# Attention heads computed transposed, with denominators from a block of ones

## The reference

```python
# x: (64, 64, 128); HEADS = 8, DIM_QK = 64, dv = 16, n = 64
qk = x @ W_qk
q, k = jnp.split(qk, 2, axis=-1)
v = x @ W_v
...
dots = jnp.einsum('bhid,bhjd->bhij', q, k) * SCALE
bias = conv[:, dist]
attn = jax.nn.softmax(dots + bias[None], axis=-1)
out = jnp.einsum('bhij,bhjd->bhid', attn, v)
out = out.transpose(0, 2, 1, 3).reshape(b, n, h * dv)
return out @ W_out + b_out
...
x = _layernorm(x + _L0_attn_ref(...), axis=-1)
```

## Time and profile before

| | |
|---|---|
| median of 3 runs | 484.66 us |
| lowest, highest | 481.88, 485.7 us |
| profiled execution, its own time | 484.01 us |
| its span in the trace | 482.3 us |
| mean granted TensorE clock | 0.975 of full speed |
| instructions in the span | 14464 |

### The profile page before, as it was taken

One profiled execution on the slowest core, in us unless ns is written; L12 is line 12 of the kernel. 1 busy time (PEld: TensorE's weight loads), 2 busy tenths in 40 slices (PEclk: granted clock), 3 DMA queues, 4 the chain that ended last, 5 costly groups with the idle time before them and its releaser, 6 DMA issues.

```text
span 482.3 us, 14464 instructions
## 1 busy us (share of the span) xinstructions
PE 446.0 (92%) x5114; PEld 377.0 (78%) x5115; DVE 308.0 (64%) x993; ACT 301.1 (62%) x675; POOL 185.6 (38%) x209
## 2 busy tenths in 40 slices
PE   8999999999988999999889999988888999899984
PEld 7688888888877767666558999887877999899631
DVE  5578888888886578878875687433333544445246
ACT  5677877787675989978678745443435664232236
POOL 5522022208100111127556556366564666554300
PEclk9999999999998999999988999998898999999998
DMA  5342226700000061111121242122212232211186
GB/s 143 88 125 77 77 59 125 212 3 3 12 14 24 23 220 46 45 34 59 56 72 47 80 116 78 29 68 66 75 56 72 71 82 79 79 51 35 56 302 199
DMA packets 47485, 38.05 MB, mean 79 GB/s; under 512 B 5056, under 2 KB 40784, under 8 KB 47424
## 3 DMA queue, kind: packets, MB, share of 16 engines
q1 hardware_dynamic: 42672, 28.10, 21.2%
q0 software_dynamic: 4320, 8.92, 5.6%
q10 hardware_dynamic: 432, 0.20, 0.2%
HBM read 19.30 MB, written 16.34 MB: 74 GB/s over the span
## 4 chain that ended last, share of the span: by engine, by line
PE 54%; DVE 21%; ACT 10%; issue 6%; another core or an unknown queue 3%; DMA 3%; DVEq 1%; SPq 0%; ACTq 0%; POOL 0%; POOLq 0%
PE bank L1418 9%; PE bank L1332 6%; PE bank L1376 4%; PE bank L1386 3%; PE bank L1405 3%; PE bank L1407 2%; PE bank L1406 2%; DVE tkr L1541 2%; DVE negmax L1550 2%; DVE prob L1547 2%; PE bank L1056 2%; PE bank L1003 2%; PE bank L1005 2%; PE bank L1004 2%
## 5 line engine op out<-in xcount | busy, mean ns | idle before, releaser
L593 POOL DMA_INDIRECT routed<-rh,zbuf x71 | 74.1, 1043 | 60.5 <-DVE rh L1926 34.7
L1926 DVE TENSOR_SCALAR rh<-bank,zbuf 128x128 f32<-128x128 f32 x71 | 24.8, 349 | 53.2 <-PE bank L1418 20.2
L1418 PE MATMUL bank<-wdn,prob 128*128 x400 | 52.0, 285 | 1.1 <-issue 1.0
L1418 PEld LDWEIGHTS bank<-wdn,prob 128*128 128x128 f32 x400 | 49.8, 201 | 1.7 <-issue 1.4
L928 ACT ACTIVATE prob<-bank 128x512 f32<-128x512 f32 x50 | 29.3, 597 | 25.9 <-remote 12.0
L1405 PE MATMUL bank<-xT_hi,wq_hi 128*128 128x256 f32 x100 | 31.6, 316 | 9.9 <-ACT prob L928 7.4
L490 POOL DMA_INDIRECT slots<-zbuf,slot x32 | 31.7, 989 | 21.9 <-PE bank L1332 8.7
L490 POOL DMA_INDIRECT slots<-tkr,slot x32 | 31.6, 989 | 12.4 <-issue 6.7
L480 POOL TENSOR_TENSOR hlw<-hst,lnw 128x512 f32<-128x512 f32 x8 | 10.2, 1274 | 63.2 <-ACT hst L803 63.2
L913 ACT ACTIVATE prob<-bank 128x512 f32<-128x512 f32 x21 | 12.5, 597 | 31.1 <-PE bank L1376 29.1
L1332 PEld LDWEIGHTS bank<-sdn,qblk 128*128 128x128 f32 x256 | 30.1, 194 | 0.6
(11 more groups left out here) (303 smaller groups left out, 1228.6 us busy)
## 6 DMA issues: line engine op xcount, KB each, us to landing
slots<-x2T SPq DMA_DIRECT2D x8, 585.0 KB, 5.2
zbuf<-slots SPq DMA_DIRECT2D x25, 130.0 KB
tkr<-in_x SPq DMA_DIRECT2D x8, 256.0 KB, 3.1
cs<-in_ctx SPq DMA_DIRECT2D x8, 256.0 KB, 2.9
wup<-in_L_ffn_routed_up SPq DMA_DIRECT2D x1, 2048.0 KB, 8.4
zbuf<-tkr SPq DMA_DIRECT2D x8, 256.0 KB
wup<-routed SPq DMA_DIRECT2D x8, 256.0 KB, 3.7
wdn<-routed SPq DMA_DIRECT2D x8, 256.0 KB, 4.3
```

What stands on the lines that cost most here:

```text
L593: pool.indirect_dma_start(routed, bass.IndirectOffsetOnAxis(ap=xr[n][:, :].bitcast(I32)[:, DEST:DEST + 1], axis=0), yr[n % 4][:, :], None) ...
L1418: m = mm(bank[6 + a][:, 0:D], hTp[:, q, c // 2, c % 2, a, :], wdn[:, bass.ds(e * (FC * D) + c * D, D)], start=(c == 0), stop=(c == FC - 1))
L1926: tsc(yr[n % 4][:, :], bank[6 + n % 2][:, 0:D], xr[n % NX][:, GATE:GATE + 1], None, ALU.mult).then_inc(s["y_ok"], 1)
```

## The change

The weights of `heads` are now the values, and the probabilities move through them, so that the result comes out transposed, with the eight heads' 16 value columns on the 128 partitions and the tile's 128 tokens in the columns. Four matmuls with the weights `dblk` (128x32, ones for the head of each half, zeros elsewhere) go ahead of the eight: they give the denominator of each head and token once on each of that head's 16 rows. VectorE then takes the reciprocal of this 128x128 block, and multiplies the 128x128 sums by it, directly into `oT`, which now has two buffers. `out_turn`, `oT_evac`, `o`, `o_ok` and `oT_ps` are gone; `proj` waits for VectorE in place of ScalarE. `vblk` has lost its columns of ones.

```diff
-    vblk = sb("vblk", [P, GT * 8, 2, DV + 1])
-    rden = sb("rden", [P, GT, H])
-    o = sb("o", [P, D])
-    oT = sb("oT", [P, P])
+    vblk = sb("vblk", [P, GT * 8, 2, DV])
+    dblk = sb("dblk", [P, 2, DV])
+    rden = sb("rden", [P, P])
+    oT = [sb(f"oT{n}", [P, P]) for n in range(2)]
...
-        def oT_evac(g, k):
-            act.wait_ge(s["oT_ps"], GT * g + k + 1)
-            act.activation(oT[:, :], bank[2 + k % 2][:, 136:136 + P], ACT.Copy).then_inc(s["oT_ok"], 1)
...
         def proj(g, k):
             pe.wait_ge(s["oT_ok"], GT * g + k + 1)
-            mm(bank[2 + k % 2][:, 264:264 + D], oT[:, :], wo[:, :], start=True, stop=True).then_inc(s["pr_ps"], 1)
-
-        def out_turn(g, k):
-            pe.wait_ge(s["o_ok"], GT * g + k + 1)
-            pe.transpose(bank[2 + k % 2][:, 136:136 + P], o[:, :], ident[:, :]).then_inc(s["oT_ps"], 1)
+            mm(bank[2 + k % 2][:, 264:264 + D], oT[k % 2][:, :], wo[:, :], start=True, stop=True).then_inc(s["pr_ps"], 1)
...
             for j in range(4):
-                for a in range(2):
-                    m = mm(bank[2 + k % 2][a * S:(a + 1) * S, j * 34:j * 34 + 34],
-                           probT[:, j * P + a * S:j * P + a * S + S],
-                           vblk[:, k * 8 + a * 4 + j, :, :], start=True, stop=True)
+                mm(bank[2 + k % 2][j * 2 * DV:(j + 1) * 2 * DV, P:2 * P], dblk[:, :, :], probT[:, j * P:(j + 1) * P],
+                   start=True, stop=True)
+            for a in range(2):
+                for j in range(4):
+                    m = mm(bank[2 + k % 2][j * 2 * DV:(j + 1) * 2 * DV, a * S:(a + 1) * S], vblk[:, k * 8 + a * 4 + j, :, :],
+                           probT[:, j * P + a * S:j * P + a * S + S], start=True, stop=True)
             m.then_inc(s["av_ps"], 1)
...
-            u = bank[2 + k % 2][:, 0:136].rearrange("p (h d) -> p h d", h=H)
-            st(dve.reciprocal(rden[:, k, :], u[:, :, DV]))
-            tt(o[:, :].rearrange("p (h d) -> p h d", h=H), u[:, :, 0:DV],
-               spread(rden[:, k, :], [P, H, DV]), ALU.mult).then_inc(s["o_ok"], 1)
+            st(dve.reciprocal(rden[:, :], bank[2 + k % 2][:, P:2 * P]))
+            tt(oT[k % 2][:, :], bank[2 + k % 2][:, 0:P], rden[:, :], ALU.mult).then_inc(s["oT_ok"], 1)
```

More of the change, by code:

```diff
@@ L241, in decoder_layer @@
     const_p const_v wq_ok read_ok gwT_ps gw_ok vsteps xT_ps xT_ok xhi_ok xlo_ok
-    wqlo_ok z_ps z_ok s_ps v_ps v_ok logit_ok exp_ok pT_ps pT_ok av_ps o_ok oT_ps oT_ok pr_ps
+    wqlo_ok z_ps z_ok s_ps v_ps v_ok logit_ok exp_ok pT_ps pT_ok av_ps oT_ok pr_ps
     res_ok stat_ok mv_ok lnv_ok rstd_ok x1_ok asteps cs_ok x1T_ps x1T_ok cT_ps cT_ok g_ps
@@ L649, in v_evac @@
                 r = slice(half * S, half * S + S)
-                act.activation(vblk[r, :, half, 0:DV], bank[7][r, :].rearrange("p (n d) -> p n d", d=DV),
+                act.activation(vblk[r, :, half, :], bank[7][r, :].rearrange("p (n d) -> p n d", d=DV),
                                ACT.Copy).then_inc(s["v_ok"], 1)
@@ L693, in group_a @@
             if not first:
-                oT_evac(g - 1, 2)
                 pT_evac(g - 1, 3)
@@ L703, in group_a @@
             v_evac(g, first)
-            if not first:
-                oT_evac(g - 1, 3)
             pT_evac(g, 0)
@@ L715, in group_a @@
             pT_evac(g, 1)
-            oT_evac(g, 0)
             if front:
@@ L730, in group_a @@
             pT_evac(g, 2)
-            oT_evac(g, 1)
             if more:
@@ L769, in _ @@
         pT_evac(NG - 1, 3)
-        oT_evac(NG - 1, 2)
         maxima(0)
-        oT_evac(NG - 1, 3)
         rsqrt_a(NG - 1)
@@ L1066, in group_a @@
                 values(g)
-                out_turn(g - 1, 2)
             if not first:
@@ L1086, in group_a @@
             prob_turn(g, 0)
-            if not first:
-                out_turn(g - 1, 3)
             if more:
@@ L1099, in group_a @@
             prob_turn(g, 1)
-            out_turn(g, 0)
             if more:
@@ L1115, in group_a @@
             prob_turn(g, 2)
-            out_turn(g, 1)
             if more:
@@ L1183, in _ @@
         prob_turn(NG - 1, 3)
-        out_turn(NG - 1, 2)
         pe.wait_ge(s["read_ok"], NT)
@@ L1189, in _ @@
         proj(NG - 1, 2)
-        out_turn(NG - 1, 3)
         turn_x(1)
@@ L1499, in _ @@
         st(dve.memset(vblk[:, :, :, :], 0.0))
-        st(dve.memset(vblk[0:S, :, 0, DV:DV + 1], 1.0))
-        st(dve.memset(vblk[S:P, :, 1, DV:DV + 1], 1.0))
+        st(dve.memset(dblk[:, :, :], 0.0))
+        st(dve.memset(dblk[0:S, 0, :], 1.0))
+        st(dve.memset(dblk[S:P, 1, :], 1.0))
         dve.wait_ge(s["xhi_ok"], 1)
```

## The result

Five runs of each kernel on one chip: the changed kernel took 499.48 us in the median (497.98 to 501.77), the kernel before 485.7 us (481.88 to 487.89). The ratio is 1.029, with a 95% interval of 1.0247 to 1.0333: slower by 2.9%. The profiled execution took 497.98 us with a span of 496.2 us, 13.9 us more than before; its mean granted TensorE clock was 0.977.

A forecast was written before the change was run, and what follows sets the result against it. With the slow reciprocal, VectorE alone was to bound attention's loop; start 1.8, loop 16.3, end 3.5 less 0.6 gave +21.0 us on the profiled 484.01, so 505 us, range 490 to 512.

The forecast's parts named there:

- The forecast case: Attention: a slow reciprocal at 4 to 9 ns a column, no change of clock, 490 to 512 us; chance 0.80.
- What bounds the kernel: Attention's loop: VectorE and TensorE both within some 5% of full; VectorE works 15.37 of 16.19 us a turn, waits 0.82.
- The reciprocal: VectorE, each of 32 tiles: 128 columns at 7.4 ns each take 1.09 us, adding 0.885 us a tile.
- The loop: Six turns of attention: VectorE alone the bound at 18.91 us a turn, 2.72 us more each, 16.3 us in all.
- The start: Attention ahead of the loop: a wait of 1.45 us swallows the first reciprocal's addition, the next two count, 1.8 us.
- The end: Attention behind the loop: five reciprocals less waits add 3.5 us; VectorE's idle time before the last residual goes, -0.6.
- TensorE: Each tile: new `heads` 0.66 us, against 0.71 before for old `heads` and one transpose; gains 0.05 us a tile.
- ScalarE, the product, the memsets at nothing: Attention: the copies gone from ScalarE, shorter way to `proj` in the loop, VectorE's product at 0.291 us and memsets change nothing.
- Rival 1: VectorE's reciprocal streams: 128 columns take 0.33 us, a turn changes by +0.15 us, 484.5 us in all; chance 0.15.
- Rival 2: TensorE is the bound: reciprocal streams, but narrow `heads` passes take 37 ns each; +4.6 us, 489; chance 0.02.
- Rival 3: TensorE's clock falls to half in the loop as it waits in each tile: some 25 us on top, 530; chance 0.03.

The follow-up runs named there:

- e5: Kernel before with its reciprocal widened to 136 columns and GpSimd's pair held back until VectorE's layer norm is written: 507.18 us, ratio 1.0489 to the kernel before.
- e12: Changed kernel with the inverse on ScalarE, residual ahead of product on VectorE and GpSimd's pair held back: 461.93 us, ratio 0.9942 to the kernel before.

## Why the prediction was right, and where its sizes were off

The forecast case came in: slower, by a slow reciprocal that makes VectorE the bound. The measured 499.48 is 5.5 us below 505, within the range. By its steps:

- **What bounds the kernel.** Right in kind. I took VectorE's waits from the idle times shown, 0.82 us a turn. But where VectorE doesn't wait, such an instruction starts up to 0.08 us before the end of the one ahead (the product at 67.70 above takes 0.29 us, and the next starts at 67.91), and the idle time counts from that end; a wait of 0.30 shown pushes the next start by some 0.38. Read between starts, the two waits were 0.99 us, and VectorE's own work 15.20, not 15.37. With the measured reciprocal, 15.20 + 4 x 0.747 = 18.19; the trace has 18.17. The other half of the picture, that below the bound two of the four `head_out`s set the turn, gave 16.7 us for 64 columns, where 16.98 were measured.
- **The reciprocal**, the term that matters. Right in kind (a price per column, from an excess of 51 ns over eight columns), 7.4 ns taken, 6.25 measured; 0.952 us, not 1.09, and +0.747 us a tile, not +0.885. The reduction that I subtracted was too cheap a stand-in for the fixed part; the copy of eight columns, had the trace had one, gives 6.4. The Trainium skill's page "VectorE: DVE Perf Modes", section "First, the fixed hardware budget", has a repeat count of eight, from which I had estimated 8.3 ns and some 508 us; the runs don't agree with it as a price per column, since 6.25 ns is six cycles at that page's 0.96 GHz.
- **The loop.** 16.3 us predicted, 11.7 measured. Of the 0.74 us a turn between 2.72 and 1.98, 0.55 is the price and 0.17 the waits. "The waits go and VectorE alone is the bound" held at 128 columns.
- **The start.** 1.8 us predicted, 0.49 measured: the largest miss for its size. I let the wait of 1.45 us swallow one reciprocal and counted the next two. It did swallow the first: the wait is 0.80, and the second reciprocal even starts 0.27 us earlier than before (27.28 against 27.55), which takes part of its own cost. The third one's was given back by something that I had not seen in the trace of before. There one subtraction of 0.69 us took 1.53, behind GpSimd's instruction that began 0.20 us ahead of it; after, the same subtraction begins 0.96 us after GpSimd's, near its end, and takes 0.78.

```profile
...
30.26 1.53 DVE L1551 TENSOR_TENSOR prob<-prob,negmax 128x512 f32<-128x512 f32 x1
...
```

```profile
...
30.06 1.18 POOL L417 TENSOR_TENSOR tkr<-tkr,bout 128x512 f32 x1
```

```profile
...
30.75 0.78 DVE L1532 TENSOR_TENSOR prob<-prob,negmax 128x512 f32<-128x512 f32 x1
...
```

- **The end.** 3.5 - 0.6 = 2.9 us predicted, 1.75 measured. With 0.747 us for each of the five reciprocals the same sum is 3.7 - 0.9 - 0.6 = 2.2; three waits that were under-read by 0.08 us each take 0.2 more; 0.2 stay open. That the idle time ahead of the last residual goes came true.
- **TensorE.** `heads` 0.58 us, not 0.66: the 8 passes of 128 columns took 0.24 (0.22 taken), the 16 of 64 columns 0.34 (0.44 taken), 21 ns each, near the low bound; the transposes of `prob` to the next instruction fell by 0.11 (0.12 predicted). It hid behind VectorE, as the prediction had it. The wait for `pair`, once a turn, was not foreseen and cost nothing, as TensorE has time over.
- **ScalarE, the product, the memsets at nothing.** The product is 0.292 us; right. "Nothing" for the shorter way to `proj` holds where the reciprocal is short; e5 shows that with a long one the old way costs a wait.
- **Rival 1** (it streams) falls by the reciprocals of several lengths, and with it the reading of a divide that gives a result each cycle; the run with 8 columns shows about what it would have brought, 0.9965. **Rival 2** falls with the same run. **Rival 3** falls: the loop ran at full clock with TensorE 85% busy. After a wait of 2.51 us at the end it stayed there too, where the earlier trace rows had it at half after 1.31; why, the runs don't tell.

## What to carry to other kernels

Price an instruction by two lengths of it before it is widened: a reciprocal that took 0.2 us at eight columns was the longest instruction of the tile at 128, and to replicate a denominator before the division, rather than after, multiplies the dearest operation by the replication. Work given to an engine in a loop costs at least what exceeds its waits there, so read these waits between starts, not from the idle times; it can cost more, since with 64 columns the turn grew by 1.00 us for 1.4 us of work and a wait stayed. And when a change shifts an engine's timing, look at what another engine does at the new time: here VectorE against GpSimd lengthened a turn by 1.8 us in one version and by 0.94 in another, and one wait on GpSimd took the latter from the same time as the kernel before to 0.6% less.

## What the runs showed of the hardware

A reciprocal costs 6.25 ns a column from 8 to 512 columns, from PSUM and SBUF alike (3357 and 3353 ns for 512); a copy from PSUM 1.04 ns.

A VectorE instruction that reads two operands in SBUF (0.69 us for 128x512) and the TENSOR_SCALARs from SBUF to SBUF (1.11 us for four) grew beside a GpSimd instruction with two SBUF operands: the one to 1.53 to 1.71 us where GpSimd's had started ahead, the four to 2.97 us. GpSimd's takes 1.64 in place of 1.19 us when VectorE's started ahead. The addition of the bias, one of whose operands is in PSUM, stood at 0.69 us beside it (at 65.18 in e12, where GpSimd's instruction of 1.19 us had started at 65.12). The Trainium skill has this in "SBUF — State Buffer", section "Who interferes with whom": a VectorE instruction with two SBUF inputs, or in a two-port mode, contends with a GpSimd instruction that reads SBUF for a shared pair of ports, which is an exclusive lock, and the order of issue decides who blocks. These traces agree for the instruction with two inputs, in both orders of start; whether the TENSOR_SCALARs ran in a two-port mode they don't show.
